# One turn over five PSUM banks for relation products and halves of count products, and counts spread over all 196 quads

## The reference

```python
h_src = h_hc[src]                      # gathered node rows
r_uv  = r_hc[edge_type]                # relation rows, 500 relations
m = clifford_linear(h_src * r_uv, msg_w, msg_b) * gate * norm
h_agg = segment_sum(m, dst)
h_out = clifford_linear(h_hc + h_agg, upd_w, upd_b)
x = layernorm(x + h_out)
...
mean_nb = segment_sum(x[src], dst) / max(deg, 1)      # three times
h = relu(mean_nb @ Wl.T + bl + x @ Wr.T)
```

## Time and profile before

| What | us |
|---|---|
| Median of 3 runs | 3438.51 |
| Lowest and highest | 3432.74 and 3440.49 |
| The profiled execution | 3430.29 |
| Its span, first to last instruction | 3428.4 |
| Busy: TensorE, GpSimd, VectorE, ScalarE | 2885.8, 2417.4, 2429.2, 2133.6 |
| Mean granted clock | 0.91 |

### The profile page before, as it was taken

One profiled execution on the slowest core, in us unless ns is written; L12 is line 12 of the kernel. 1 busy time (PEld: TensorE's weight loads), 2 busy tenths in 40 slices (PEclk: granted clock), 3 DMA queues, 4 the chain that ended last, 5 costly groups with the idle time before them and its releaser, 6 DMA issues. The chain is left out here.

```text
span 3428.4 us, 53365 instructions
## 1 busy us (share of the span) xinstructions
PE 2885.8 (84%) x16283; PEld 2485.7 (73%) x16283; DVE 2429.2 (71%) x5400; ACT 2133.6 (62%) x3761; POOL 2417.4 (71%) x2281
## 2 busy tenths in 40 slices
PE   5569888888888888889589999768999976899995
PEld 4468777777777777778377878657787855778884
DVE  7878777777777777787466666546666654677786
ACT  1066776666666666666377777447777735777772
POOL 6277777777766777776477777767777757777773
PEclk7589999999999999999699999979999987999998
DMA  4255555555555555556566666466666637666663
GB/s 135 79 147 162 163 152 146 154 155 148 143 150 147 154 155 144 157 153 167 171 189 184 194 189 194 138 211 191 186 196 186 196 105 238 193 203 200 206 201 97
DMA packets 327862, 572.43 MB, mean 167 GB/s; under 512 B 47877, under 2 KB 225878, under 8 KB 327574
## 3 DMA queue, kind: packets, MB, share of 16 engines
q0 software_dynamic: 105696, 290.56, 30.9%
q1 hardware_dynamic: 218361, 275.92, 25.7%
q10 hardware_dynamic: 3517, 2.48, 0.3%
HBM read 494.21 MB, written 74.56 MB: 166 GB/s over the span
## 5 line engine op out<-in xcount | busy, mean ns | idle before, releaser
L1476 POOL DMA_INDIRECT rows_arena<-table_h,src_idx x1224 | 1301.5, 1063 | 466.3 <-issue 369.0
L1476 POOL DMA_INDIRECT rows_arena<-table_scaled_x,src_idx x782 | 847.3, 1084 | 378.1 <-issue 255.3
L2039 PE MATMUL bank<-wide_counts,h_pairs 128*128 128x512 f32 x3528 | 874.6, 400 | 0.0
L1976 PE MATMUL bank<-rel_pairs,ftype_hot 125*128 125x258 f32 x4688 | 755.5, 312 | 51.2 <-ACT ftype_hot L1602 50.8
L2039 PEld LDWEIGHTS bank<-wide_counts,h_pairs 128*128 128x128 f32 x3528 | 660.6, 193 | 136.8 <-DVE h_pairs L1821 0.3
L1976 PEld LDWEIGHTS bank<-rel_pairs,ftype_hot 125*128 125x128 f32 x4688 | 666.4, 204 | 84.0 <-ACT ftype_hot L1602 50.9
L1813 DVE TENSOR_TENSOR row_pairs<-rows_arena,row_pairs 128x1024 fp32r<-128x1024 f32 x306 | 373.3, 1220 | 443.2 <-ACT row_pairs L1611 440.8
L1611 ACT CAST row_pairs<-rows_arena 128x1024 fp32r<-128x1024 f32 x306 | 320.3, 1047 | 462.9 <-DMA rows_arena<-table_h,src_idx 454.5
L1999 PE MATMUL bank<-row_pairs,rel_pairs 128*128 128x256 f32 x2448 | 392.5, 306 | 186.0 <-DVE row_pairs L1813 185.7
L1623 ACT CAST wide_counts<-rows_arena 128x1024 fp32r<-128x1024 bf16 (+1 forms) x450 | 501.9, 1115 | 0.0
L1999 PEld LDWEIGHTS bank<-row_pairs,rel_pairs 128*128 128x128 f32 x2448 | 339.6, 203 | 218.4 <-issue 213.6
(11 more groups left out here) (186 smaller groups left out, 3101.5 us busy)
## 6 DMA issues: line engine op xcount, KB each, us to landing
rows_arena<-edge_counts SPq DMA_DIRECT2D x234, 512.0 KB, 4.0
edge_counts<-fcount SPq DMA_DIRECT2D x48, 832.0 KB, 6.4
rows_arena<-in_edge_type_dram SPq DMA_DIRECT2D x195, 187.5 KB
rows_arena<-table_h,src_idx POOLq DMA_INDIRECT x1224, 3.6
rows_arena<-table_h SPq DMA_DIRECT2D x36, 512.0 KB, 11.9
rows_arena<-table_scaled_x,src_idx POOLq DMA_INDIRECT x782, 3.7
table_h<-chunk_info SPq DMA_DIRECT2D x96, 128.0 KB, 4.2
rows_arena<-in_x_dram SPq DMA_DIRECT2D x6, 1024.0 KB
```

The costliest lines, as they stand in the source:

```text
L1476: pool.indirect_dma_start(out=rows[:, g % ring, c, :], out_offset=None, in_=table[:, :], in_offset=bass.IndirectOffsetOnAxis(ap=src_idx[:, ...
L1976: last = pe.matmul(relation_bank[r % 3][:, 0:RW], type_hot[:, g % 2, kk, i * P:(i + 1) * P], rel_pairs[:, kk, part, :], start=(kk == 0 and ...
L2039: last = pe.matmul(bank[2 + h][:, 0:PASS_COLS], h_pairs[:, v % HALVES, part, b % HALF, h * P:(h + 1) * P], wide_counts[:, v % HALVES, b % ...
```

## The change

All relation products and all halves of count products of layer 0 are put in one list, `in_turn`, in the order in which TensorE makes them, and take banks 0, 1, 7, 2 and 3 in fixed turn. Each waits for the reader of the product five places earlier: a message of VectorE where that was a relation product, a copy of ScalarE where it was half a count. The count's semaphores `s_count` and `s_staged` now count halves, so ScalarE copies a half when that half is there, and each half's matmul has its own wait and its own increment. `COUNTS_EARLY` is gone: the counts are spread over the positions of all 196 quads. No instruction that computes is added or removed.

```diff
-                return [i for i in range(ND if first else 0) if i * 2 * (NG - COUNTS_EARLY) // ND == position]
+                return [i for i in range(ND if first else 0) if i * 2 * NG // ND == position]
...
+            in_turn = []
+            for g in range(NG if first else 0):
+                for i in range(GC):
+                    if i < chunks_of(g) - len(pool_rel(g)):
+                        in_turn.append(("relation", products(g) + i))
+                    if i in (0, 2):
+                        in_turn += [("count", 2 * j + h) for j in counts_at(2 * g + i // 2) for h in range(2)]
+            place = {of: u for u, of in enumerate(in_turn)}
...
-                relation_bank = [bank[0], bank[1], bank[7]]
+                turn_banks = [bank[0], bank[1], bank[7], bank[2], bank[3]]
...
+                    return turn_banks[place[what, n] % len(turn_banks)]
...
-                            act.wait_ge(s_count, i + 1)
                             if i >= STAGES:
                                 act.wait_ge(s_counted, i - STAGES + 1)
                             for h, (lo, hi) in enumerate(halves):
-                                last = act.copy(staged[:, i % STAGES, lo:hi, :].rearrange("p t w -> p (t w)"),
-                                                bank[2 + h][:, 0:(hi - lo) * KEY_W])
-                            last.then_inc(s_staged, 1)
+                                act.wait_ge(s_count, 2 * i + h + 1)
+                                act.copy(staged[:, i % STAGES, lo:hi, :].rearrange("p t w -> p (t w)"),
+                                         bank_of("count", 2 * i + h)[:, 0:(hi - lo) * KEY_W]).then_inc(s_staged, 1)
...
+                        def bank_read(what, n):
+
+                            u = place[what, n] - len(turn_banks)
+                            if u < 0:
+                                return
+                            before, m = in_turn[u]
+                            if before == "relation":
+                                quad, chunk = made[m]
+                                pe.wait_ge(s_msg, GC * quad + chunk + 1)
+                            else:
+                                pe.wait_ge(s_staged, m + 1)
...
-                            if r >= 3:
-                                before, chunk = made[r - 3]
-                                pe.wait_ge(s_msg, GC * before + chunk + 1)
+                            bank_read("relation", r)
...
-                            if i:
-                                pe.wait_ge(s_staged, i)
                             for h, (lo, hi) in enumerate(halves):
-                                last = pe.matmul(bank[2 + h][:, 0:(hi - lo) * KEY_W], lo_hot[:, i % COUNT_HOTS, :],
-                                                 key_hot[:, i % COUNT_HOTS, lo * KEY_W:hi * KEY_W], start=True, stop=True)
-                            last.then_inc(s_count, 1)
+                                bank_read("count", 2 * i + h)
+                                pe.matmul(bank_of("count", 2 * i + h)[:, 0:(hi - lo) * KEY_W], lo_hot[:, i % COUNT_HOTS, :],
+                                          key_hot[:, i % COUNT_HOTS, lo * KEY_W:hi * KEY_W], start=True, stop=True
+                                          ).then_inc(s_count, 1)
```

More of the change, by code:

```diff
@@ L65 @@
 EARLY = 10
-COUNTS_EARLY = 6
 HC = 8
@@ L1451, in one_round_layer, with bank_of @@
                 turned_h = bank[6][:, 0:D]
+                def bank_of(what, n):
+                    return turn_banks[place[what, n] % len(turn_banks)]
                 def rows_full(g):
@@ L1741, in message @@
                                 dve.wait_ge(s_rel_mm, r + 1)
-                                relation = relation_bank[r % 3][:, 0:D + 1]
+                                relation = bank_of("relation", r)[:, 0:D + 1]
                             dve.tensor_tensor(msg[:, g % MSGS, c, 0:D + 1], relation,
@@ L1778, in count_hots @@
                             if i >= COUNT_HOTS:
-                                dve.wait_ge(s_count, i - COUNT_HOTS + 1)
+                                dve.wait_ge(s_count, 2 * (i - COUNT_HOTS + 1))
                             slot = i % COUNT_HOTS
@@ L1796, in count_add @@
                             at_col = dve.value_load(chunk_at[0:1, i:i + 1], min_val=0, max_val=(COUNT_RING - 1) * HTILE)
-                            dve.wait_ge(s_staged, i + 1)
+                            dve.wait_ge(s_staged, 2 * i + 2)
                             if i:
@@ L1970, in relation @@
                             r = products(g) + i
-                            if r >= 3:
-                                before, chunk = made[r - 3]
-                                pe.wait_ge(s_msg, GC * before + chunk + 1)
+                            bank_read("relation", r)
+                            rows_bank = bank_of("relation", r)
                             for kk in range(RK):
                                 for part in range(2):
-                                    last = pe.matmul(relation_bank[r % 3][:, 0:RW],
+                                    last = pe.matmul(rows_bank[:, 0:RW],
                                                      type_hot[:, g % 2, kk, i * P:(i + 1) * P],
```

## The result

The changed kernel takes 3380.45 us (median of 4 runs, 3372.55 to 3385.18), the kernel before 3437.94 us (3432.74 to 3440.49). The ratio is 0.9832 with a 95% interval of 0.981 to 0.9855: 58 us less, 50 to 65. The profiled executions took 3430.3 and 3382.2 us, 48 us apart.

What follows compares the result with a forecast made beforehand. Layer 0's quads were taken to be bound by a ring of waits, with VectorE late before each stall. Terms -37 - 15 + 2 + 0 = -50 us gave 3388 against the median 3438.5, own case 3370 to 3410 (0.58).

Steps and rivals of the forecast that it cites:

- The ring: In layer 0's quads TensorE waits for ScalarE, ScalarE for VectorE, VectorE for TensorE; VectorE's 98.6 us caps the gain.
- Term 1: Stalls in layer 0's quads: count pair runs inside the stall, relation 1 needs one half copied; 37 us less.
- Term 2: Stalls in layer 0's quads: 13 fewer end at lower clock, 1.2 us each; 15 us less, bounds 0 and 35.
- Term 3: Count products: one more wait and increment on TensorE, one more wait on ScalarE; +2 us, between 0 and +7.
- New waits for messages: TensorE ahead of counts waits for VectorE's messages, 31.4 and 10.7 us, covered by the stall behind; costed at 0.
- The slower rival: Ahead of the second count, new message waits push TensorE behind: +53 us, 3491; chance 0.08.
- Term 4: Twelve counts move from slots 0 to 189 to slots 190 to 195: 0 us, between -7 and +5.
- VectorE has no use for it: Stall moves to relation 1, VectorE's saved waits reappear at degrees, sums or value loads: 3432 to 3445; chance 0.12.
- The gathers become the bound: Layer 0's gathers need 1312.8 us; rows late for message 0 give back about half: 3405 to 3420; chance 0.10.
- The expected marks: Profile after, over the quads: copy wait about 100 us, messages 30 to 45, VectorE about 50, gather queue about 75.

Runs made afterwards that it cites:

- e8: Kernel before, with only ScalarE's square root of a block moved behind the slot's two count copies: 3321.79 against 3435.74 us, ratio 0.9678.
- e12: Changed kernel with TensorE waiting for the copies of both halves of a count wherever it waits for one: 3404.36 us, ratio 0.9907.
- e3: Kernel before with waits, copies and increments by half, count banks 2 and 3 fixed, no turn: ratio 0.9985 (0.9967 to 1.0003).
- e11: Changed kernel with ScalarE's square root moved behind the slot's two count copies: 3318.76 against 3434.14 us, ratio 0.9671.
- e7: Kernel before with the change's waits for VectorE's messages added ahead of the counts: ratio 0.997 (0.993 to 1.001).
- e1: Changed kernel with counts over 190 quads as before, the turn without the spread: 3941.75 against 3959.2 us, ratio 0.9962.
- e2: Kernel before with counts spread over all 196 quads and nothing else: ratio 1.0013 (0.9991 to 1.0036).
- e10: Changed kernel without the relation table's second part, four matmuls per relation product: 3360.13 us, ratio 0.9797 to the kernel before.
- e5: The changed kernel again, unaltered, on a slower chip: 3947.14 against 3951.96 us for the kernel before, ratio 0.997.

## Why the prediction was right, step by step

**The ring and who is late.** Right, and e8 shows it more plainly than the change does: moving nothing but the square root undoes the stalls and gives 111 us. The prediction took VectorE's 98.6 us of waits for products as the most that can come back. That holds for the turn. In e8 the quads are 121 us shorter: VectorE's waits for products fell by 93 us, its 19.7 us before the take (L1856, for ScalarE's degree root) to 0.6, its waits for copies and clears of counts by 15, and its busy time by 16, while 17 us of waits for gathered rows and 8 us of idle time before count additions came in.

**Term 1, 37 us.** Its two parts were 0.6 us for the pair and 0.39 for half a copy. Slot 70 shows 0.86 us less from the start of the copies to the start of the relations: 0.39 of it for the pair (703.86 to 704.25) and 0.47 for the half copy (1.04 less 0.57). So the sum was near, with the pair taken too high and the half too low. By e12 the half is worth 26 us where 39 x 0.39 = 15 was reckoned; 39 x 0.47 would be 18, and e12 also spends about 26 us more at 1.2 GHz in the quads than the change, so a part of the 26 belongs to term 2. What remains for the turn with whole counts, 32 us with its own clock falls, fits the 29 x 0.6 + 10 x 0.37 = 21 reckoned for the pair and a part of term 2.

**Term 2, 15 us.** Thirteen fewer stalls followed by the lower level were expected. In the record of the clock, of TensorE's idle times over 1 us (whatever it waits for) about 30 of 48 were followed by it before and about 17 of 55 after, and the time at 1.2 GHz in the quads fell from about 181 us to 93. So the count was right. What each is worth was not measured by itself: no kernel here has the old stalls at the full clock. Terms 1 and 2 together are 52 in the prediction and 53 in the quads of the profiles, and they can only be checked as a sum. That these two agree so closely is partly luck: both terms were to come out of VectorE's waits for products, which fell by 44, not 52. The rest is small changes that the prediction did not have, less busy time (8 us) and shorter idle times before count and window additions (some 19), against waits that grew elsewhere (17).

**Term 3, +2 us.** e3 has all the added waits and increments and is at most 1 us slower than the kernel before, at the upper end of its interval, with whatever the earlier half gives already taken off. e11, which has them too, is at most 8 us slower than e8 on chips at about 3435 us. So the 2 us can't be told from nothing. The 26.3 ns for an increment, which the Trainium skill's page "TensorE: Matmul & The Clock Gate", section "The cost: per-tile semaphore tail", states for tiles packed into the array together, would be 9.8 us here, an estimate, if each increment lay on the path. These two comparisons speak against it, e3 by a narrow margin if its half gives the 8 us expected.

**New waits for messages, 0.** They are there as forecast, 42.0 us (31.4 + 10.7 = 42 in the prediction); that the sums agree to the digit is luck, since they are 31 waits and not 46. They cost nothing that can be told: e7 has such waits without the turn, e11 has 98 us of them. Part of their cover is the stall behind, as argued; in e11 hardly a stall for a copy is left, so there the cover must be another, probably that TensorE is not what the quads wait for. The slower rival falls with this. Nor does the clock swing under them: e11 has more than twice as many us of them and 0.99 over the quads. What the Trainium skill's section "A second HAM failure mode: psum-queue depth-cycling", on the same page, tells of another kernel isn't borne out by this turn.

**Term 4, 0.** e1 and e2 bear it out, within some 10 us, on a chip at 3959 us.

**The other rivals.** "VectorE has no use for it" is wrong where the kernel before takes 3440 us: its wait fell by 44 us. But some of it did come back as this rival said: the wait for the degree root rose from 19.7 to 27.2 us and the one for count copies from 24.9 to 34.9. With light relation products (e10) most of it does. "The gathers become the bound" came a step later: not for the change (67.7 us of the queue's waits are left), but, by the gather queue's rows, for e8.

**The expected marks.** TensorE's wait at the relation line 84 us (about 100 expected), messages 42 (30 to 45), VectorE 54 (about 50), gather queue 68 (about 75), clock 0.96, last relation product at 1576 (quads near 1580). From the last relation product on it is 4 us more, not the same. The measured 58 us lies 8 above the 50 forecast.

**The better version.** e8 and e11 beat both kernels by far (3322 and 3319 us). e8 needs neither the turn nor the spread.

## What to carry to other kernels

Where an engine stands idle, follow the chain to the instruction that its releaser stood at, here a square root of 0.2 us that sat ahead of two copies in ScalarE's list. Here moving it gave 111 us, and giving the waiting engine more banks 58. What a shorter stall is worth is bounded by the idle time of the engine that is late before the stall, counting all its waits in the ring, and not by the length of the stall.

## What the runs showed of the hardware that was not expected

On two chips (e1 to e7) the same program takes 3952 to 3961 us, 15% more, at a clock of about 0.87. In their traces TensorE's matmul records look as on the other chips, but its increments seem to come late. From the modelled end of a relation product to the next recorded increment of its semaphore it is 0.4 to 0.8 us in the median of each of these seven traces, and up to 12 us, against 0.014 us in the profiles of the kernel before and after. The rows "remote" above are VectorE and ScalarE waiting for semaphores of TensorE. The record itself is thinner there, though: 510 to 546 increments of that semaphore stand in it against 604 and 605, and e5's trace has 24,984 semaphore updates in all against 59,442 of the same kernel above. So a part of the delay can be increments that are missing from the record, and whether the signals or the matmuls' real ends are late isn't shown. There the turn gives 0.3 to 0.4% instead of 1.7%. What holds TensorE back on those chips stays open; no run here tells it.
